# Convolution and mixture sublayer: the experts' outputs weighed by GpSimd and folded by three additions of VectorE

## The reference

```python
def _L2_ffn_ref(x, ...):
    xc = depthwise_causal_conv(x, dw_kernel) + dw_bias          # 3 taps
    x1 = x + silu(xc @ pw_w.T + pw_b)
    logits = x1 @ router_w.T + router_b
    top_v, top_i = lax.top_k(logits, 2)
    rw = sum over the two of one_hot(top_i, E) * softmax(top_v)  # (token, E), two entries not zero
    ye = silu(einsum('bsd,eod->bseo', x1, expert_w) + expert_b)  # all 8 experts on every token
    combined = einsum('bse,bseo->bso', rw, ye)
    moe_out = combined @ out_w.T + out_b
    h = rmsnorm(x1 + moe_out, norm_w)
    ff = gelu(h @ ff_down_w.T + ff_down_b) @ ff_up_w.T + ff_up_b
    return h + ff
```

## Time and profile before

| | us |
|---|---|
| median of 3 runs | 3607.47 (3604.95 to 3610.28) |
| the profiled execution's own time | 3619.05 |
| its span, first to last instruction | 3616.9 |
| busy in the span: PE, DVE, ACT, POOL | 2818.4, 2157.7, 1818.0, 1838.9 |
| mean granted TensorE clock | 0.885 of full speed |

### The profile page before, as it was taken

The page is one execution under the profiler, slowest core; times in us unless marked ns, Lnnn a source line. Parts: engine busy times, 40 slices in busy tenths (PEclk is TensorE's granted clock), DMA queues, the critical chain, the costliest instruction groups (busy, mean ns, idle before and its releaser), DMA issues. The chain is left out here.

```text
span 3616.9 us, 83245 instructions
## 1 busy us (share of the span) xinstructions
PE 2818.4 (78%) x28638; PEld 1992.1 (55%) x28638; DVE 2157.7 (60%) x5986; ACT 1818.0 (50%) x3448; POOL 1838.9 (51%) x1774
## 2 busy tenths in 40 slices
PE   2259985698999799953529998997888779992993
PEld 2258974475666466632416665654444446662893
DVE  2101324655888688862337886777999778872124
ACT  0024543553666566611216665775567776660451
POOL 3721245544888755525465555664133755555226
PEclk9679998898999899975559999998999899995997
DMA  8246763120111111114611112221000012212584
GB/s 296 86 135 217 233 199 90 39 8 14 43 47 46 55 51 70 67 40 136 164 53 43 56 54 68 89 87 44 1 1 1 8 30 73 76 54 88 178 249 128
DMA packets 321561, 308.86 MB, mean 85 GB/s; under 512 B 110950, under 2 KB 244489, under 8 KB 320908
## 3 DMA queue, kind: packets, MB, share of 16 engines
q1 hardware_dynamic: 279644, 255.42, 22.9%
q0 software_dynamic: 16384, 33.59, 3.1%
q10 hardware_dynamic: 25264, 16.40, 1.5%
HBM read 167.28 MB, written 60.69 MB: 63 GB/s over the span
## 5 line engine op out<-in xcount | busy, mean ns | idle before, releaser
L956 DVE TENSOR_TENSOR moe_first_tile_y<-moe_first_out_ps,moe_first_expert_w 128x256 f32<-128x256 f32 x85 | 35.7, 423 | 377.7 <-PE moe_first_out_ps L1092 248.1
L1092 PE MATMUL moe_first_out_ps<-moe_first_expert_w,moe_first_hid 128*128 128x128 f32 x1360 | 181.7, 280 | 75.0 <-issue 73.5
L1092 PEld LDWEIGHTS moe_first_out_ps<-moe_first_expert_w,moe_first_hid 128*128 128x128 f32 x1360 | 174.2, 196 | 85.8 <-issue 80.2
L814 POOL DMA_INDIRECT moe_first_token_y<-slot_y,moe_first_slots x128 | 124.6, 974 | 175.0 <-DMA slot_y<-moe_first_tile_y 137.0
L1913 POOL TENSOR_TENSOR causal_k_blocks<-causal_k_T,headmask 128x1024 f32<-128x1024 f32 x64 | 121.5, 1899 | 96.5 <-PE causal_scores L1518 94.5
L1165 POOL DMA_INDIRECT slot_x<-x_tok,moe_first_slots x128 | 123.5, 965 | 87.7 <-DVE moe_first_slots L928 49.3
L1913 POOL TENSOR_TENSOR alibi_k_blocks<-alibi_k_T,headmask 128x1024 f32<-128x1024 f32 x64 | 121.3, 1898 | 91.3 <-PE alibi_scores L1518 90.0
L1913 POOL TENSOR_TENSOR full_k_blocks<-full_k_T,headmask 128x1024 f32<-128x1024 f32 x64 | 120.8, 1898 | 82.2 <-PE full_scores L1518 80.0
L3211 PE MATMUL L_ffn_experts<-weights_odd,x_T 128*128 128x512 f32 x256 | 138.1, 622 | 11.6 <-ACT L_ffn_expert_out L3311 11.5
L1913 POOL TENSOR_TENSOR keys_k_blocks<-keys_k_T,headmask 128x1024 f32<-128x1024 f32 x64 | 120.9, 1900 | 46.7 <-PE keys_scores L1518 45.6
L3134 DVE SCALAR_TENSOR_TENSOR L_ffn_combined<-L_ffn_expert_out,L_ffn_mix,L_ffn_combined 128x128 f32<-128x128 f32 x448 | 139.0, 373 | 3.9
(11 more groups left out here) (634 smaller groups left out, 9005.9 us busy)
## 6 DMA issues: line engine op xcount, KB each, us to landing
moe_first_expert_w<-in_L_attn_experts SPq DMA_DIRECT2D x85, 578.0 KB
moe_last_expert_w<-in_L_ffn_experts SPq DMA_DIRECT2D x53, 578.0 KB
moe_first_tile_x<-slot_x SPq DMA_DIRECT2D x85, 128.0 KB
slot_y<-moe_first_tile_y SPq DMA_DIRECT2D x85, 128.0 KB
slot_x<-blank ACTq DMA_DIRECT2D x2, 4992.0 KB
L_ffn_tile_x<-slot_x SPq DMA_DIRECT2D x32, 256.0 KB
slot_y<-L_ffn_tile_y SPq DMA_DIRECT2D x32, 256.0 KB
moe_last_tile_x<-slot_x SPq DMA_DIRECT2D x53, 128.0 KB
```

Source lines behind the costliest of these rows:

```text
L814: pool.indirect_dma_start(y_in[:, p, k, r, :], None, slot_y[part][0:NTS[part] * SLOT_TILE, :], bass.IndirectOffsetOnAxis(slots[:, part, r, ...
L956: dve.tensor_tensor(y_out[:, q, :, :], out_bank[j % 2][:, 0:SLOT_TILE].rearrange("p (s d) -> p s d", s=SPAN), over(wall[:, j % RING, 2 * F ...
L1092: last = pe.matmul(out_bank[j % 2][:, D * s:D * s + D], hid[:, j % 3, b, TILE * s:TILE * s + TILE], wall[:, j % RING, FF + D * b:FF + D * ...
```

## The change

`combine` is split over two engines. GpSimd gets a stage `weigh`, first in its list, which multiplies `expert_out` in place by `mix`, spread over the 128 outputs: one TENSOR_TENSOR of 128 x 1024 for each of the four tiles. VectorE folds the eight products by three TENSOR_TENSOR additions: 128 x 2048 (experts 0 to 3 plus 4 to 7), 128 x 1024, 128 x 512. The stage `combine` moves from the middle of VectorE's list to its end, behind `rank`, `mean_square` and `residual`; `turn_combined` moves behind the first two tiles of `experts` in TensorE's list. `mix_two` now also waits until `weigh` of two chunks before has read its buffer.

```diff
@@ vector: mix_two
+                if c >= 2:
+                    dve.wait_ge(weighed, PER * (c - 1))
                 dve.tensor_scalar(mix[:, c % 2, :, :], twice[:, :, :], 0.5, None, ALU.mult).then_inc(mix_done, 1)
@@ vector: combine
-                dve.wait_ge(mix_done, c + 1)
-                dve.wait_ge(expert_done, 2 * PER * (c + 1))
+                got = expert_out[:, p, :, :, :]
+                dve.wait_ge(weighed, PER * (c + 1))
+                dve.tensor_tensor(got[:, :, 0:4, :], got[:, :, 0:4, :], got[:, :, 4:8, :], ALU.add).then_inc(fold_steps, 1)
+                dve.wait_ge(fold_steps, 2 * c + 1)
+                dve.tensor_tensor(got[:, :, 0:2, :], got[:, :, 0:2, :], got[:, :, 2:4, :], ALU.add).then_inc(fold_steps, 1)
+                dve.wait_ge(fold_steps, 2 * c + 2)
                 if c >= 2:
                     dve.wait_ge(combT_ready, c - 1)
-                for e in range(E):
...
+                dve.tensor_tensor(combined[:, p, :, :], got[:, :, 0, :], got[:, :, 1, :], ALU.add).then_inc(comb_done, 1)
@@ vector: the list
-            return [(-4, lambda c: convolve(c) if c else None), (-1, mix_two), (-3, add_pointwise), (0, combine),
-                    (-2, rank), (2, mean_square), (5, residual)]
+            return [(-4, lambda c: convolve(c) if c else None), (-1, mix_two), (-3, add_pointwise), (-2, rank),
+                    (2, mean_square), (5, residual), (0, combine)]
@@ tensor: the list
-            return [(4, down_product), (1, turn_combined), (-3, pointwise_product), (-2, route),
-                    (-1, lambda c: experts(c, (0, 1))), (3, turn_h), (2, output), (-1, lambda c: experts(c, (2,))),
+            return [(4, down_product), (-3, pointwise_product), (-2, route), (-1, lambda c: experts(c, (0, 1))),
+                    (1, turn_combined), (3, turn_h), (2, output), (-1, lambda c: experts(c, (2,))),
@@ gpsimd
+            def weigh(c):
+                p = c % 2
+                pool.wait_ge(mix_done, c + 1)
+                for k in range(PER):
+                    pool.wait_ge(expert_done, 2 * (PER * c + k + 1))
+                    pool.tensor_tensor(expert_out[:, p, k, :, :], expert_out[:, p, k, :, :],
+                                       spread_last(mix[:, p, k, :], D), ALU.mult).then_inc(weighed, 1)
+
-            return [(4, rows_with_residual), (2, rms), (5, inverse_std)]
+            return [(0, weigh), (4, rows_with_residual), (2, rms), (5, inverse_std)]
```

More of the change, by code:

```diff
@@ L3048, in conv_moe @@
         expert_ready, expert_done = sem("experts_ready"), sem("experts_done")
-        comb_done = sem("combined")
+        weighed, fold_steps, comb_done = sem("experts_weighed"), sem("fold_steps"), sem("combined")
         combT_ready, combT_copied, z_ready, squared = sem("combT_ready"), sem("combT_copied"), sem("z_ready"), sem("squared")
@@ L3121, in combine @@
                 p = c % 2
-                dve.wait_ge(mix_done, c + 1)
-                dve.wait_ge(expert_done, 2 * PER * (c + 1))
+                got = expert_out[:, p, :, :, :]
[4 more added lines that the diff above has]
+                dve.wait_ge(fold_steps, 2 * c + 2)
                 if c >= 2:
                     dve.wait_ge(combT_ready, c - 1)
-                for e in range(E):
-                    if e:
-                        dve.wait_ge(comb_done, E * c + e)
-                    for k in range(PER):
-                        w = mix[:, p, k, e:e + 1]
-                        if e == 0:
-                            last = dve.tensor_scalar(combined[:, p, k, :], expert_out[:, p, k, e, :], w, None, ALU.mult)
-                        else:
-                            last = dve.scalar_tensor_tensor(combined[:, p, k, :], expert_out[:, p, k, e, :], w,
-                                                            combined[:, p, k, :], ALU.mult, ALU.add)
-                    last.then_inc(comb_done, 1)
+                dve.tensor_tensor(combined[:, p, :, :], got[:, :, 0, :], got[:, :, 1, :], ALU.add).then_inc(comb_done, 1)
             def mean_square(c):
@@ L3217, in turn_combined @@
             def turn_combined(c):
-                pe.wait_ge(comb_done, E * c + E)
+                pe.wait_ge(comb_done, c + 1)
                 if c >= 1:
@@ L3307, in experts_silu @@
                     if c >= 2:
-                        act.wait_ge(comb_done, E * (c - 1))
+                        act.wait_ge(comb_done, c - 1)
                     for g in range(2):
```

## The result

The changed kernel took 3618.64 us (median of 10 runs, 3611.62 to 3629.19), the kernel before, run beside it, 3604.69 (10 runs, 3600.17 to 3611.73): a ratio of 1.0042, 95% interval 1.0029 to 1.0054, slower by 0.42% or 14 us; the profiled execution took 3624.73 us around a span of 3622.2. The forecast was 3631 us, slower by 24. The sign and the mechanism stand; the size is about half of what the sum gave, and the experiments show a second limit beside the one I forecast, which I had costed at nothing.

A forecast was written before the change was run, and what follows sets the result against it. VectorE's queue was taken to set the step, TensorE 3 us behind. Terms of +16.3, +3.6, +6.5 and -2.5 us gave +23.9, rounded +24, on the median of 3607.47: 3631 us, range 3604 to 3660.

The forecast's parts named there:

- six full steps: Steps with every stage at work: 19.58 us less 4.76 saved plus 6.8 held, so +2.04 us each.
- two steps of 17.9: The two steps of 17.87 us, costed like the full ones at +2.04 us each.
- three early steps: First steps, some products beside `rank`: between +0.3 and +2.0 us each, taken as +1.2, together +3.6.
- four late steps: Steps without the convolution: `combine` waits for GpSimd's last product, 17.9 instead of 16.28 us, together +6.5.
- the ends: The last `combine` no longer has `mean_square` and `residual` of its step behind it: about -2.5 us.
- The start: GpSimd's products in a full step start near 5.5 us after the end of VectorE's moments.
- The hold: Each GpSimd product holds up VectorE's operations by 1.7 us, between 1.62 and 1.90: 6.8 us a chunk.
- All seven are spent before VectorE reaches `rank`: In a full step, GpSimd's four products and three other wide operations all meet VectorE's eleven susceptible operations ahead of `rank`.
- I cost both moves at nothing: Moving `combine` and `turn_combined` is free: the loop over TensorE has 5 us of slack in a 21.6 us step.
- Rival 1: Products run beside VectorE operations that are not held up, from `rank` to the moments: faster, 3566 us; chance 0.09.
- Rival 2: Some three of the four products are held up, so no change: 3607 us, give or take 7; chance 0.10.
- Rival 3: A product takes 2.3 us instead of 1.90, held up by VectorE: 26 us more, 3657; chance 0.15.

The follow-up runs named there:

- e7: Changed kernel with GpSimd's products behind its two rows' operations and held back until VectorE has added the pointwise product, to run beside `rank`: ratio 0.9994 to the kernel before.
- e1: Kernel before with the two moves alone, `combine` last on VectorE and `turn_combined` behind two tiles of `experts`, no products on GpSimd: 3687.64 us.
- e6: Kernel before with VectorE's move alone, the 32 operations of `combine` last in its list, TensorE's order untouched: ratio 1.0333.
- e11: Changed kernel with one 128x4096 product on VectorE instead of GpSimd's four, and `residual` with its moments behind `combine`: ratio 0.9983 to the kernel before.
- e3: Changed kernel with each GpSimd product replaced by three fills of 128x680 that read nothing, same waits: 3609.69 us.
- e4: Changed kernel with `combine` and `turn_combined` back at their old places, products still on GpSimd: 3638.54 us.
- e9: Changed kernel with TensorE's move alone undone, `turn_combined` back ahead of the pointwise product and `experts`: ratio 1.0073 to the kernel before.

## Why the prediction was right in sign and too high

**The terms.** The sum was +23.9 us; the stretch grew by 10.4.

| term | predicted | measured |
|---|---|---|
| six full steps | +12.2 | +5.2 |
| two steps of 17.9 | +4.1 | +4.9 |
| three early steps | +3.6 | +2.5 |
| four late steps | +6.5 | +1.2 |
| the ends | -2.5 | +4.8 - 5.6 - 2.5 = -3.3 |

**Right.** The additions: 2.26, 1.23 and 0.69 us, from 2688.14 to the convolution at 2692.30 is 4.16 for the predicted 4.25, where 9.01 was. The products: 1.89 at least, median 1.945, four of them 7.99 in the step shown. The start: the products begin 5.5 us behind the moments, as forecast. The hold: over their own durations the operations beside the four products lose 6.53 us, 1.63 each (predicted 1.7 between 1.62 and 1.90), one small operation slipping in between two. GpSimd's wait for `mean_square` fell from 67.9 us to 6.8 in six steps. TensorE waits more: 17.6 us in six steps, 2.9 each, for ScalarE, which waits for the additions, where it waited 2.4 each for `combined`.

The Trainium skill's rule (SBUF — State Buffer, Who interferes with whom) is a hold of the whole instruction, and the prediction made 7.6 us a chunk of it. The trace agrees with the rule and not with that sum: each of the three small operations that are held ends 0.04 to 0.05 us after the product beside it, so it does wait to the product's end. VectorE still loses only 6.53 of the products' 7.99 us, because the held operation's own work, and that of the small one ahead of it, is done within the product's time or lengthens the next product: the second product of the step waits for the convolution's operation and takes 2.32.

**The ends, near by luck.** The sum had -2.5 for what no longer stands behind the last `combine`, and that is what it is: from the end of the last `combine` to the last `residual` 35.1 us for 37.6. Two terms are missing in it. The first `combine` comes 4.8 us later behind the first convolution, and the last `combine`, which no step between starts contains, is itself 5.6 us shorter (7.06 for 12.68). They nearly cancel.

**The full step, mis-sized.** "All seven are spent before VectorE reaches `rank`" is the step that failed: six are. `h_plus_x` falls beside `rank` and no longer stretches anything, where before it held the first operation of `combine` (1.29 us in the trace of before); that is one hold of 1.0 us less. The prediction's own count could have shown it: of its eleven operations the first two pass before 5.5 us, and one hold for each of seven wide operations with a small one between leaves too few of the other nine. With it, and from the steady 19.74 instead of a mean of 19.58 that had a shorter step in it, the prediction's own sum closes: 19.74 - 4.85 + 6.53 - 1.0 = 20.4. e7 bears it out: with two operations held by the products instead of four VectorE is busy for 96.52 us of six full steps instead of 119.72, and the step falls to the 18.5 us that GpSimd needs.

**The moves, wrong in their slack and without consequence here.** "I cost both moves at nothing" with 5 us of slack. e1 shows that they cost 6 us a step where the combination is long, e6 that it is VectorE's move, e11 that the way is through `residual`, which my loop named. Its length was what I had not worked out: it is 13.2 us in e3 beside the combination, so with the additions' 4.2 some 17.4 in a full step of the changed kernel's 20.4: 3 us of slack, not 5. The changed kernel shows it itself: in its first step without a convolution, from the `combine` at 2749.45 to the one at 2766.83, VectorE waits 1.67 us for `up_ps` and the step is 17.38. The move was free because the shorter combination came with it, and because the products had made VectorE's own queue longer than the loop; with the products on GpSimd it is even needed (e4's full step is 21.8). This also bounds what the products' holds cost in a full step: without them (e3) the loop and VectorE's stretched additions give 19.9 us, half a microsecond less.

**The late steps, mis-sized by a drift.** GpSimd's step there does cost 17.67 us (from 2781.69 to 2799.36), near the 17.9 of the sum, but `combine` feels it only once GpSimd is late. The products of chunk 12 ended 4.4 us ahead of their `combine` (`x_res` behind them begins at 2762.42, `combine` at 2766.83), those of chunk 13 3.8, of chunk 14 2.2, and only those of chunk 15 are waited for:

```profile
2815.73 3.36 DVE L3126 TENSOR_TENSOR L_ffn_expert_out<-L_ffn_expert_out 128x2048 f32<-128x2048 f32 x1 [1.97 <-POOL L_ffn_expert_out L3402]
```

Until then the loop sets the step, 17.4 us in the first and 16.2 and 16.1 in the next two, where VectorE comes to wait for the squares:

```profile
2794.79 0.69 DVE L3138 TENSOR_REDUCE L_ffn_ms<-L_ffn_z_sq 128x4 f32<-128x512 f32 x1 [6.28 <-ACT L_ffn_z_sq L3320]
```

I multiplied an engine's longer step by four steps, where the slack of some 4 us ahead of it had to be used up first.

**The two steps of 17.9** are 0.8 us above the sum and the three early ones 1.1 below; no experiment was made on either.

**The rivals.** Rival 1 (the products beside what isn't held up) didn't happen, for the reason given, the place in GpSimd's order; e7, which puts them there, gains in the full steps and not over the whole. The rival's 3566 had no loop in it: at 17.4 us in full steps and 16.1 in late ones it stands above the 16.5 and 14.3 that the rival took. Rival 2 (some three of the four held up) didn't either: in a full step all four products hold an operation. Rival 3 would have needed products of 2.3 us; their median is 1.945, and in the step shown one of the four takes that long.

## What to carry to other kernels

In this case the move in a queue had its price through the loop that it closed. So write down the chain from the end of the moved stage back to its next start with its length, and add the stage's own duration: the same moves cost 82 us with 32 operations in the stage, and with three the loop stayed below the queue that set the step. Work given to another engine is not gone where both engines delay each other: four products of 1.9 us cost VectorE 6.5 us, more than the 4.4 us of the one product when VectorE does it itself. When an engine gets slower by x a step, subtract the slack ahead of its reader before multiplying by the steps.

## What the runs showed of the hardware

- Beside GpSimd's products VectorE's operations fall into two kinds whatever their size. Held to the product's end: TENSOR_TENSOR of 128x4 (1.89 us for 0.15), CAST of 128x8 (1.83 for 0.17), both in e7. At their own durations: the TENSOR_REDUCE of the squares, the `residual` sum with `up_ps`, the BATCH_NORM operations. So the smallest operation of the first kind can cost as much as a large one.
- Fills of GpSimd, which read nothing, leave VectorE's operations of two inputs alone: in e3 two SCALAR_TENSOR_TENSOR take 1.52 us beside them (at 2550.22) and `shifted` 0.15; with a product beside them these take 3.18 in the changed kernel and 1.89 in e7. By the Trainium skill (SBUF — State Buffer, Who interferes with whom) a VectorE instruction with two SBUF inputs contends with a GpSimd instruction that reads SBUF and not with one that only writes it; e3 agrees. A CAST (0.43 us for 0.17) and a TENSOR_SCALAR (up to 0.56 for 0.18) are held by the fills as well.
- VectorE holds GpSimd up too: L611 of 128x4 takes 2.18 us beside the addition of 2048, 0.43 in the earlier trace rows.
- After waits of TensorE its granted clock is at the lower level, 0.50 (1.2 GHz): in e9 for 8.6 us, behind 4.3 us in which it was busy for 1.05, and in e1 behind a wait of 7.20 us, where its first two pairs of matmuls take 2.08 and 1.91 us for 1.02 later in the step. These pairs stand in the loop, so some 2 us of e1's 14.2 beside the combination (1.06 and 0.89 in these two rows) come from the clock. In e3, with a shorter wait, one of the two pairs takes 1.91; its loop is 13.2.
